# A graph network on one core: the second gather adds into the first one's rows, and VectorE's add of the two goes

## The reference

```
msg_s = (s_n @ Ws_src)[src] + (s_n @ Ws_dst)[dst]
msg_v = einsum('ncx,cd->ndx', v_n, Wv_src)[src] + einsum('ncx,cd->ndx', v_n, Wv_dst)[dst]
w1 = rbf @ W_rbf
m1_s, m1_v = tensor_product(msg_s, msg_v, y0, y1, w1)     # products, a dot and a cross product
a = sum(leaky(m1_s @ W_alpha) * alpha_dot)                # attention logits, 4 heads
val_s, val_v = m1_s @ Ws_val, (m1_v @ Wv_val) * sigmoid(val_s @ Wg)
m2_s, m2_v = tensor_product(sigmoid(val_s), val_v, y0, y1, w2)
h = (m2_s @ Ws_vlin, m2_v @ Wv_vlin)                      # what is later summed with softmax(a)
```

## Time and profile before

| | us |
|---|---|
| median of three runs (8192.76 to 8199.45) | 8196.07 |
| the profiled execution | 8192.76 |
| its span | 8190.9 |
| VectorE busy | 5909.9 |
| TensorE busy | 6392.7 |
| GpSimd busy | 4872.1 |
| first and last gather of the changed phase start at | 1623.4 and 4175.3 |

### The profile page before, as it was taken

The page is one execution under the profiler, slowest core; times in us unless marked ns, Lnnn a source line. Parts: engine busy times, 40 slices in busy tenths (PEclk is TensorE's granted clock), DMA queues, the critical chain, the costliest instruction groups (busy, mean ns, idle before and its releaser), DMA issues. The chain is left out here.

```text
span 8190.9 us, 152807 instructions
## 1 busy us (share of the span) xinstructions
PE 6392.7 (78%) x33102; PEld 4646.5 (57%) x33103; DVE 5909.9 (72%) x13214; ACT 2171.6 (27%) x5890; POOL 4872.1 (59%) x5664
## 2 busy tenths in 40 slices
PE   2999999478888888888863388868888887888886
PEld 0555557177777777777751166654555554555555
DVE  3799995488888888888864422256887863788884
ACT  3000001055555555555550011130000001000001
POOL 1677773076666666666647755525666651777771
PEclk9999999599999999999985589978998986899998
DMA  4233331243333333333310033312232321222221
GB/s 166 77 86 86 85 86 47 63 117 109 109 109 109 110 110 109 109 110 109 110 55 0 0 96 102 104 51 71 81 81 80 81 71 35 74 74 75 75 75 40
DMA packets 517234, 683.80 MB, mean 83 GB/s; under 512 B 140977, under 2 KB 360817, under 8 KB 517042
## 3 DMA queue, kind: packets, MB, share of 16 engines
q0 software_dynamic: 193920, 384.17, 18.0%
q1 hardware_dynamic: 323250, 298.86, 11.8%
HBM read 579.47 MB, written 103.21 MB: 83 GB/s over the span
## 5 line engine op out<-in xcount | busy, mean ns | idle before, releaser
L882 POOL DMA_INDIRECT e_rows<-tab,e_idx x2424 | 2366.0, 976 | 1129.3 <-issue 719.3
L1154 POOL DMA_INDIRECT acc<-tabx,a_idx x1616 | 1724.7, 1067 | 1127.6 <-issue 465.9
L910 PE MATMUL e_win<-e_feat,e_ohy 128*128 128x320 f32 (+1 forms) x4848 | 1743.8, 507 | 26.4 <-DVE e_feat L994 26.0
L910 PEld LDWEIGHTS e_win<-e_feat,e_ohy 128*128 128x128 f32 x4848 | 963.4, 207 | 649.8 <-issue 453.3
L922 PE MATMUL e_wps<-e_w,e_hidT 64*128 64x192 f32 (+1 forms) x4848 | 1028.7, 355 | 345.0 <-DVE e_hidT L999 339.7
L922 PEld LDWEIGHTS e_wps<-e_w,e_hidT 64*128 64x128 f32 x4848 | 828.4, 193 | 614.3 <-DVE e_hidT L999 485.9
L1207 PE MATMUL a_tps<-ident_sb,acc 128*128 128x128 f32 (+1 forms) x4848 | 789.0, 288 | 365.3 <-DVE acc L1310 229.1
L1207 PEld LDWEIGHTS a_tps<-ident_sb,acc 128*128 128x128 f32 (+1 forms) x4848 | 546.6, 143 | 515.5 <-issue 513.4
L1211 PE MATMUL a_c<-acc 128*128 128x128 f32 (+1 forms) x4848 | 742.4, 293 | 114.1 <-ACT acc L1190 113.4
L1211 PEld LDWEIGHTS a_c<-acc 128*128 128x128 f32 (+1 forms) x4848 | 653.7, 204 | 147.0 <-issue 147.0
L994 DVE TENSOR_TENSOR e_feat<-e_wps,e_rows 128x384 f32<-128x384 f32 x1414 | 708.2, 548 | 0.0
(11 more groups left out here) (221 smaller groups left out, 9277.7 us busy)
## 6 DMA issues: line engine op xcount, KB each, us to landing
h_d<-acc SPq DMA_DIRECT2D x202, 320.0 KB, 2.4
s_hin<-h_d SPq DMA_DIRECT2D x202, 320.0 KB, 3.3
e_rows<-tab,e_idx POOLq DMA_INDIRECT x2424
e_ein<-in_e64T SPq DMA_DIRECT2D x202, 128.0 KB
acc<-tabx,a_idx POOLq DMA_INDIRECT x1616
a_ein<-e_part SPq DMA_DIRECT2D x404, 48.0 KB
e_ein<-e_part SPq DMA_DIRECT2D x202, 96.0 KB
e_part<-s_parts SPq DMA_DIRECT2D x36, 404.0 KB, 3.1
```

Source lines behind the costliest of these rows:

```text
L882: pool.indirect_dma_start(out=rows[:, s, t, :], out_offset=None, in_=k.tab0, in_offset=bass.IndirectOffsetOnAxis(ap=idx[:, s, t:t + 1], ax ...
L910: mm = pe.matmul(win[:, s, 0:NF], ohy[:, s, t, :, :].rearrange("p y n -> p (y n)"), feat[:, s, t, :], start=t == 0, stop=t == TPG - 1)
L1154: pool.indirect_dma_start(out=rows[:, b, q, :], out_offset=None, in_=table, in_offset=bass.IndirectOffsetOnAxis(ap=idx[:, b, end, q:q + 1] ...
```

## The change

The four target gathers of a group no longer write a buffer of their own. They write `msg` with `compute_op=ALU.add`: the DMA adds each gathered row to the row that is there. The buffer `far` and the add at the head of VectorE's `head` go, so `HEAD` is 9 and the waits within `head` count one less. Since the adding gathers may only start when the plain ones of the same buffer have landed, GpSimd's step is laid out anew: in step g it gathers the source rows of g + 4, then waits for those of g + 3 and issues the adding gathers of g + 3; it begins four steps early (`before=4`). SyncE no longer waits for `src_in` before it loads indices, as `dst_in` implies it. VectorE's `head` waits for `dst_in` alone.

```diff
-    HEAD, MID, TAIL = 10, 13, 2
+    HEAD, MID, TAIL = 9, 13, 2
...
-        msg, far = scratch(U, TPG, XD), scratch(U, TPG, XD)
+        msg = scratch(U, TPG, XD)
...
-                            hold(sp, k, src_in[b], uses(s, i, 1) * (16 * TPG) + 16 * TPG)
                             hold(sp, k, dst_in[b], uses(s, i, 1) * (16 * TPG) + 16 * TPG)
...
                 def step(g, s, i):
-                    b = s
-                    if not isinstance(g, int) or g >= U:
-                        hold(pool, k, head_ops, (g - U + 1) * HEAD)
-                    hold(pool, k, idx_in[b], i * 16 + 16)
-                    for rows, table, end, signal in ((msg, k.tabx0, 0, src_in), (far, k.tabx1, 1, dst_in)):
+                    if inside(g + 4, n):
+                        b = s
+                        if not isinstance(g, int) or g >= 0:
+                            hold(pool, k, head_ops, (g + 1) * HEAD)
+                        hold(pool, k, idx_in[b], uses(s, i, 4) * 16 + 16)
                         for q in range(TPG):
                             pool.indirect_dma_start(
-                                out=rows[:, b, q, :], out_offset=None, in_=table,
-                                in_offset=bass.IndirectOffsetOnAxis(ap=idx[:, b, end, q:q + 1], axis=0),
-                            ).then_inc(signal[b], 16)
-
-                rounds(pool, n, step, lo=U, U=U)
+                                out=msg[:, b, q, :], out_offset=None, in_=k.tabx0,
+                                in_offset=bass.IndirectOffsetOnAxis(ap=idx[:, b, 0, q:q + 1], axis=0),
+                            ).then_inc(src_in[b], 16)
+                    if inside(g + 3, n):
+                        b = (s + 3) % U
+                        hold(pool, k, src_in[b], uses(s, i, 3) * (16 * TPG) + 16 * TPG)
+                        for q in range(TPG):
+                            pool.indirect_dma_start(
+                                out=msg[:, b, q, :], out_offset=None, in_=k.tabx1,
+                                in_offset=bass.IndirectOffsetOnAxis(ap=idx[:, b, 1, q:q + 1], axis=0),
+                                compute_op=ALU.add,
+                            ).then_inc(dst_in[b], 16)
+
+                rounds(pool, n, step, before=4, lo=U, U=U)
...
-                    v.wait_ge(src_in[b], uses(s, i, 0) * (16 * TPG) + 16 * TPG)
-                    hold(v, k, dst_in[b], uses(s, i, 0) * (16 * TPG) + 16 * TPG)
-                    v.tensor_tensor(m, m, far[:, b, :, :], ALU.add).then_inc(head_ops, 1)
+                    v.wait_ge(dst_in[b], uses(s, i, 0) * (16 * TPG) + 16 * TPG)
...
-                    hold(v, k, head_ops, at + 1)
```

More of the change, by code:

```diff
@@ L1301, in head @@
                     v.tensor_tensor(feat[:, :, 96:160], wps[:, :, 96:160], m[:, :, 0:S], ALU.mult).then_inc(head_ops, 1)
-                    hold(v, k, head_ops, at + 3)
+                    hold(v, k, head_ops, at + 2)
                     v.tensor_reduce(red[:, :, :], t3[:, :, :, :].rearrange("p t x c -> p t c x"), AX.X, ALU.add).then_inc(head_ops, 1)
                     v.tensor_tensor(pair[:, :, :, 0:V], over(wy[:, :, S:96], 2, 3), mv[:, :, 0:3, :], ALU.mult).then_inc(head_ops, 1)
-                    hold(v, k, head_ops, at + 4)
+                    hold(v, k, head_ops, at + 3)
                     v.tensor_tensor(cr[:, :, :, :], x2[:, :, 0, :, :], x2[:, :, 1, :, :], ALU.subtract).then_inc(head_ops, 1)
-                    hold(v, k, head_ops, at + 6)
+                    hold(v, k, head_ops, at + 5)
                     v.tensor_tensor(feat[:, :, S:96], wps[:, :, 160:192], red[:, :, :], ALU.mult).then_inc(head_ops, 1)
-                    hold(v, k, head_ops, at + 8)
+                    hold(v, k, head_ops, at + 7)
                     v.tensor_tensor(pair[:, :, :, V:2 * V], over(wps[:, :, 192:224], 2, 3), cr[:, :, :, :], ALU.mult).then_inc(head_ops, 1)
```

## The result

The median of four runs is 8274.6 us, beside 8197.8 for the kernel before: ratio 1.0094, 95% interval 1.0077 to 1.0111. The forecast was 7994 us and a faster kernel; the stated range of 7965 to 8500 us holds the time only because it left room for a slower kernel (rival 2, chance 0.31). The profiled execution (8300.43 us, span 8298.6) is 26 us longer than the kernel's other runs (8274.49 to 8276.35), so sums over its rows come out about that much too long.

What follows compares the result with a forecast made beforehand. A ring through VectorE's add bound the kernel at 12.79 us a group; without it TensorE and ScalarE bind at 11.70. From 8192.76 us, -207 and +5 give 7991, plus 3.3 for the median: 7994 us, range 7965 to 8500.

Steps and rivals of the forecast that it cites:

- rival 2: GpSimd's accumulating gathers become the bound and the kernel is slower, from a price of 1.37 us on, 8243 to 8866 us; chance 0.31.
- e: On GpSimd, the time that accumulating adds to one gather; taken as under 0.15 us.
- the ring: Once a group: head ends, transposes, copies, products, tail, add, head; 12.79 us through VectorE, 11.56 without the add.
- The bound from above: On GpSimd, one accumulating gather costs as much as two gathers: e = 0.95 + 0.30 = 1.25 us.
- break-even: On GpSimd, the e at which the whole gain is eaten: 0.42 us, a price of 1.37 us beside 0.95.
- the 11.1: GpSimd's round per group before accumulating costs, 10.9 + 0.2 = 11.1 us, to which 4e is added.
- The add on the ring: VectorE's add at the start of head lies on the ring; its going takes 1.23 us a group off VectorE's round.
- TensorE's round of 11.70 us: TensorE and ScalarE passing tiles become the next bound: 12.79 - 1.09 = 11.70 us a group.
- The term 201 x 1.03 = 207 us: Gain in layer 1's phase: 1.03 us for each of 201 groups, -207 us in all.
- The start: Twelve gathers instead of eight lie ahead of VectorE's first head: +5 us, once.
- Rival 3: The DMA transfers of accumulating gathers bind, over 2.13 us of all 16 engines each; 8280 us at 2.5 us; chance 0.07.
- Rival 4: The add's time is hidden anyway by VectorE's 1.13 us a group of other waits, so the round holds 12.79; chance 0.04.

## Why the prediction was wrong

*The step that failed* is the price of an accumulating gather: "I take e under 0.15, as the nearest row is the gather itself". Measured, e is 0.65 us on average (1681 - 1031) and 0.60 at the least (1540 - 942). The argument from equal prices for 640 and 896 bytes was sound as far as it went, for half the bytes again make no difference; but it says nothing of a gather that also adds. The mechanism followed from it: with 0.65 us four times a group GpSimd takes 13.3 us and binds, and the ring from which the add had been taken no longer sets the time. The bound from above, 1.25 us, held, and e lies in the middle of the two bounds. With a break-even at 0.42 the evidence didn't favour the side that I took. Rival 2 is what happened, with its place and its signs (gaps of only 0.30, VectorE waiting for the DMA); at e = 0.65 its formula would have given 11.1 + 2.6 = 13.7 us a group, measured 13.27. The difference is in the 11.1: when GpSimd is never released by `head`, the gaps at borders of groups and of the loop (0.53 and 1.70) vanish into 0.30, so the base is 8 x 1.031 + 8 x 0.305 = 10.7. By that base the break-even would have stood at e = 0.52 and not 0.42, still under what was measured. The prediction also read the earlier trace rows too simply: of its long gathers, the one of 1.80 us at 3031.49 runs beside the add (which starts at 3031.38), but the one of 1.21 us at 3040.47 beside the products of `mid`. So the add's going gave back only part: the mean plain gather fell from 1.069 to 1.031 us, 0.3 us a group and not 0.5.

*The Trainium skill's rule* (two reads for each write, in "Collectives: The Full Stack", § The bandwidth ceiling; one core for each list of descriptors, in "GPSIMD Engine Reference", § When to use GPSIMD) pointed the right way. The DMA engines' time agrees with two reads, 2.1 times that of a plain gather. For GpSimd a doubled price would have been e = 0.95, and it is 0.65; and as a doubled list it would give an extra that goes with the rows, where by the estimate above only 160 of 598 ns do.

*The add on the ring* was right: with it gone and no new price, the kernel is 2.8 to 3.3% faster. *TensorE's round of 11.70 us as the next bound* was right in its place and up to 0.1 us too long: 11.69 and 11.58 us from the first to the last `tail`, and TensorE hardly waits for `head`. I took it from a mean over steps at a granted clock of 0.97; in all kernels whose group is 12.3 us or shorter the clock is 1.00 in this stretch, and the slow step of every four is gone. The term 201 x 1.03 = 207 us measured 234 (no add, old order) and 276 (plain gathers, new order), timed. By the rounds of the first, 201 x (12.78 - 11.69) = 220; the rest of its gain lies outside the phase.

*The start:* 8 us and not 5 (first `head` 19.8 us behind the first gather, 11.9 before), since the four gathers ahead of it that accumulate are the dear ones. The first gather itself starts 7.8 us later too (1631.1 for 1623.4); in other kernels of this order it starts from 1624.4 us on, so that is not put down to the change. *The added wait* cost nothing: L1161's waits for it are 15.2 us in 50 times, all within the gap of 0.30. *Rival 3* (transfers) is out, at 0.87 us each against a limit of 2.13. *Rival 4* (the add is hidden anyway) is out.

*Sum for the changed kernel:* from the first to the last `tail` it is 13.265 us a group for 12.783, over 201 groups 97 us. The first `tail` starts 15 us later (1688.6 for 1673.6), half of it the later first gather, and behind the last `tail` it takes 4 us less: 108, as the span grew by 107.7. The timed runs grew by 77, since the profiled execution was the long one; where in it the 26 us lie is not known.

## What to carry to other kernels

Work moved from one engine into another's instruction has to be priced on the engine that issues it; when that engine has 1.4 us of 12.8 to spare and the new price is unknown, forecast from the break-even and not from the nearest row. Before taking an instruction off a ring, look whether it can stand where its engine already waits: the add moved by one group earned 3% and cost nothing. And a mean round over steps at two levels of the clock (here 12.5 and 13.4 us) is a poor bound for a kernel in which the clock may change.

## What was not expected of the hardware

- An accumulating gather holds GpSimd for 1540 ns at the least and a plain one for 942; 519 of the 598 ns are still there with 64 rows, and none goes with the bytes.
- A gather's issue is longer beside VectorE operations whose two inputs both lie in SBUF, products as well as additions. In the kernel before, 1376 gathers with such an operation beside them take 1088 ns on average and up to 1822, and the 240 without one 946 ns and at most 1087; accumulating gathers without one never took over 1597 ns in the changed kernel, with one up to 2103. The Trainium skill, "SBUF — State Buffer" (§ SBUF: two separate sides), says that such an operation and a GpSimd operation that reads SBUF shut each other out, and tells of GpSimd kept from writing descriptors by VectorE copies in a fast mode; here it was plain float operations, beside gathers whose row indices lie in SBUF.
- TensorE's granted clock in the phase rose from 0.97 to 1.00 in the kernels where it waited less, and fell to 0.94 in the changed one, where it waited more. They go together in these runs; which brings the other along was not tried.
